# Attention scores transposed and taken by pairs of query tiles, with the low halves on GpSimd

## The reference, cut to what matters

```
x = x + tanh(((modulated x) @ weight @ aux1 @ aux2) + bias)
Q2, K2 = x @ Wq2 + bq2, x @ Wk2 + bk2
V = concat(cond, x) @ Wv + bv
A = softmax(Q2 @ K2.T / 16) - alpha * softmax(Q1 @ K1.T / 16)
x = x + quantised_ffn(A @ V)
```

## Time and profile before

| | |
|---|---|
| median of 3 runs | 240.14 us (239.92 to 242.85) |
| the profiled execution's own time | 242.43 us |
| its span | 240.5 us |
| attention stage, 57.26 to 190.33 us | 133.07 us |
| TensorE busy in the span | 230.2 us (96%) |
| VectorE, ScalarE, GpSimd busy | 149.8, 121.9, 70.9 us |

### The profile page before, as it was taken

One profiled execution on the slowest core, in us unless ns is written; L12 is line 12 of the kernel. 1 busy time (PEld: TensorE's weight loads), 2 busy tenths in 40 slices (PEclk: granted clock), 3 DMA queues, 4 the chain that ended last, 5 costly groups with the idle time before them and its releaser, 6 DMA issues.

```text
span 240.5 us, 3882 instructions
## 1 busy us (share of the span) xinstructions
PE 230.2 (96%) x1455; PEld 188.7 (78%) x1455; DVE 149.8 (62%) x325; ACT 121.9 (51%) x222; POOL 70.9 (29%) x97
## 2 busy tenths in 40 slices
PE   7987999999999999999999999999999899998994
PEld 7977899988997899989999899889999544433342
DVE  0744322887466557855886546546555597999963
ACT  2567603666324444345344434445435669944932
POOL 8340910444000000480663400000000065663850
PEclk9999968999999999999999999999999999999999
DMA  5990019000000000000000000000000000000044
GB/s 182 301 337 13 0 34 329 24 0 3 0 0 0 3 0 0 3 0 3 3 0 0 3 0 0 3 1 0 3 0 3 1 0 0 3 0 0 0 172 177
DMA packets 7105, 9.61 MB, mean 40 GB/s; under 512 B 800, under 2 KB 4912, under 8 KB 7088
## 3 DMA queue, kind: packets, MB, share of 16 engines
q1 hardware_dynamic: 6624, 9.11, 11.0%
q10 hardware_dynamic: 144, 0.26, 0.4%
q0 software_dynamic: 320, 0.01, 0.1%
HBM read 7.28 MB, written 2.10 MB: 39 GB/s over the span
## 4 chain that ended last, share of the span: by engine, by line
PE 81%; DVE 10%; issue 4%; ACT 2%; POOL 2%; POOLq 0%; DVEq 0%
PE ps L1017 54%; PE ps L1164 6%; DVE hmax L860 4%; PE ps L1347 3%; PE ps L1064 3%; PE ps L1001 2%; PE ps L1299 2%; DVE hid L855 2%; PE ps L1047 1%; PE ps L1204 1%; PE ps L1373 1%; PE ps L1009 1%; PE ps L1103 1%; POOL hid L980 1%; DVE hi L902 1%
## 5 line engine op out<-in xcount | busy, mean ns | idle before, releaser
L1017 PE MATMUL ps<-vh,pth 128*128 128x256 f32 x128 | 37.3, 292 | 0.3 <-DVE ptl L605 0.3
L1017 PE MATMUL ps<-vl,pth 128*128 128x256 f32 x128 | 36.1, 282 | 0.0
L1017 PE MATMUL ps<-vh,ptl 128*128 128x256 f32 x128 | 36.1, 282 | 0.0
L480 ACT ACTIVATE prob<-ps,small 128x1024 f32<-128x1024 f32 x16 | 17.8, 1115 | 21.7 <-DVE small L750 21.7
L495 ACT ACTIVATE outT<-ps,small 128x128 f32<-128x128 f32 x32 | 10.0, 366 | 33.7 <-PE ps L1204 33.7
L1017 PE MATMUL ps<-x1h,xh 128*128 128x512 f32 x64 | 26.2, 409 | 0.0
L748 DVE TENSOR_REDUCE small<-ps 128x1 f32<-128x1024 f32 x16 | 19.6, 1222 | 10.1 <-PE ps L1017 9.9
L1017 PE MATMUL ps<-x1h,xl 128*128 128x512 f32 x64 | 25.2, 393 | 0.0
L1017 PEld LDWEIGHTS ps<-vh,pth 128*128 128x128 f32 x128 | 24.4, 191 | 0.9 <-issue 0.9
L1017 PE MATMUL ps<-x1l,xh 128*128 128x512 f32 x64 | 25.0, 390 | 0.0
L1017 PEld LDWEIGHTS ps<-vl,pth 128*128 128x128 f32 x128 | 24.5, 191 | 0.0
(11 more groups left out here) (226 smaller groups left out, 557.2 us busy)
## 6 DMA issues: line engine op xcount, KB each, us to landing
result<-yst SPq DMA_DIRECT2D x8, 256.0 KB, 2.1
xn<-in_x SPq DMA_DIRECT2D x4, 256.0 KB, 5.9
xn<-in_x SPq DMA_DIRECT2D x2, 512.0 KB, 9.2
wdn<-in_L_ffn_w_down SPq DMA_DIRECT2D x1, 704.0 KB, 7.4
wgn<-in_L_ffn_w_gate SPq DMA_DIRECT2D x1, 640.0 KB, 4.4
wun<-in_L_ffn_w_up SPq DMA_DIRECT2D x1, 640.0 KB, 5.3
a<-in_L_ffn_aux_weight SPq DMA_DIRECT2D x2, 256.0 KB, 6.2
wvf<-in_L_cond_Wv SPq DMA_DIRECT2D x1, 512.0 KB, 10.8
```

Of the source, the lines that this page charges most:

```text
L480: act.activation(prob[:, j % 2, :], ps[:, 2 * (j % 2):2 * (j % 2) + 2, :], ACT.Exp, bias=col("nb", j % 2), scale=ATT_SCALE, accum_out=col( ...
L1017: last = pe.matmul(dst, a, b, start=(n == 0), stop=(n == len(passes) - 1))
```

## The change

Two query tiles make a pair (`QP` = 256 queries, `NP` = 8 pairs). Scores are computed transposed: keys on the partitions, queries along the columns, so that no transpose of the probabilities is needed. The softmax subtracts one maximum for each query, which now lies along the columns: DVE first takes the maximum over the eight key tiles (`key_max`), two transposes bring it to the queries (`key_max_T`), DVE finishes it (`query_max`), two transposes of a broadcast column spread it over the partitions (`spread_top`), and DVE subtracts it from the scores into SBUF (`distances`). ACT takes the exponential there in place and copies the high half; GpSimd subtracts for the low half, except for three of the four pieces of the last pair, which DVE does. The sum of the exponentials comes from a column of ones beside the values. All 16 values are made before the loop. The quantisation of the weights on GpSimd is cut in six parts, behind the low halves of pairs 2 to 6.

```diff
+            def scores(g, between={}):
+                for k in range(TPB):
+                    if g >= 1 and k % 2 == 0:
+                        pe.wait_ge(d_ready, 4 * (g - 1) + k // 2 + 1)
+                    if k in between:
+                        between[k]()
+                    t = slice(k * P, (k + 1) * P)
+                    last = three_passes(ps[:, k // 2, k % 2 * QP:(k % 2 + 1) * QP],
+                                        [(x1h[:, b, c, t], x1l[:, b, c, t], queries(xh, g, c), queries(xl, g, c))
+                                         for c in range(DC)])
+                    if k % 4 == 3:
+                        last.then_inc(s_ps, 1)
...
+            for g in range(1, NP):
+                scores(g, {4: lambda: do_extra(("out", g - 2))} if g >= 2 else {})
+                if g in after_scores:
+                    do_extra(after_scores[g])
+                attend(g - 1, {(0, 15): lambda: key_max_T(g), (1, 3): lambda: spread_top(g)})
+                if g in after_attend:
+                    do_extra(after_attend[g])
+            for item in at_end[:-2]:
+                do_extra(item)
+            attend(NP - 1, {(1, 12): lambda: do_extra(("tile", 0))})
+            do_extra(("tile", 1))
```

The work of ScalarE and VectorE:

```diff
+            def softmax(g):
+                for k in range(4):
+                    act.wait_ge(d_ready, 4 * g + k + 1)
+                    act.activation(prob[:, 2 * k:2 * k + 2, :], prob[:, 2 * k:2 * k + 2, :], ACT.Exp,
+                                   scale=ATT_SCALE).then_inc(p_ready, 1)
+                    if k == 0 and g >= 2:
+                        act.wait_ge(o_ps, 2 * (g - 1))
+                    act.wait_ge(p_ready, 4 * g + k + 1)
+                    copy(pth[g % 2][:, 2 * k:2 * k + 2, :], prob[:, 2 * k:2 * k + 2, :], pth_ready)
...
+            def key_max(g, h):
+
+                dve.wait_ge(s_ps, 2 * g + h + 1)
+                ins = dve.tensor_reduce(kmax[:, h, :], flat(ps[:, 2 * h:2 * h + 2, :]).rearrange("p (k q) -> p q k", k=4),
+                                        X_AXIS, ALU.max)
+                if h:
+                    link(ins)
+                    dve.tensor_tensor(kmax[:, 0, :], kmax[:, 0, :], kmax[:, 1, :], ALU.max).then_inc(kmax_ready, 1)
...
+                key_max(g, 1)
+                if g in after_scores:
+                    extra_lo(after_scores[g])
+                query_max(g)
+                distances(g)
+                if g >= 2:
+                    out_max(("out", g - 2))
+                attention_out(g - 1)
+                if g <= IC:
+                    ffn_weight_scales((g - 1) // 2, (g - 1) % 2)
```

After its last softmax ScalarE reads up 0, and then the items of `at_end`. GpSimd:

```diff
+            def prob_lo(g):
+                for k in range(4):
+                    if low_half_on(g, k) == "pool":
+                        pool.wait_ge(pth_ready, 4 * g + k + 1)
+                        pool.tensor_tensor(ptl[:, g % 2, 2 * k:2 * k + 2, :], prob[:, 2 * k:2 * k + 2, :],
+                                           pth[g % 2][:, 2 * k:2 * k + 2, :].bitcast(F32),
+                                           ALU.subtract).then_inc(ptl_ready["pool"], 1)
+
+            for g in range(NP):
+                prob_lo(g)
+                for m in {2: [0], 3: [1], 4: [2], 5: [3], 6: [4, 5]}.get(g, []):
+                    k, part = m // 2, m % 2
+                    n = (IC if k < 2 else DC) // 2
+                    ffn_weight(k, range(part * n, (part + 1) * n), n)
```

More of the change, by code:

```diff
@@ L116, in build_block, with low_half_on, low_halves @@
               (3, 4, "act", "act")]
+    def low_half_on(g, k):
+        return "dve" if g == NP - 1 and k > 0 else "pool"
+    def low_halves(g, k, engine):
+        return sum(low_half_on(i, j) == engine for i in range(g + 1) for j in range(4) if (i, j) <= (g, k))
     def rounded_upto(piece, engine):
@@ L484, in probT_hi @@
[L484 to L492, removed]
+                copy(vh[:, v, 0:D], ps[:, bank, 0:D], vh_ready)
+            def softmax(g):
[7 more added lines that the diff above has]
+                    copy(pth[g % 2][:, 2 * k:2 * k + 2, :], prob[:, 2 * k:2 * k + 2, :], pth_ready)
@@ L502, in extra_read @@
                     query_hi(item[1], item[2], ps[:, MISC, :])
-                elif item[0] == "value":
-                    value_hi(item[1], MISC)
+                elif item[0] in ("out", "tile"):
+                    out_hi(item)
                 else:
@@ L753, in probT_lo @@
[L753 to L766, removed]
@@ new lines, in _ @@
+            dve.wait_ge(x1T_ready, DC * NH)
+            rank_one_vectors()
+            for v in range(NT):
+                if v == 4:
+                    key_max(0, 0)
+                    rank_one_columns()
+                    key_max(0, 1)
+                value_lo(v, value_bank(v))
+                if v == 9:
+                    dve.wait_ge(vl_ready, 2)
+                    query_max(0)
+            distances(0)
+            extra_lo(after_scores[0])
+            key_max(1, 0)
+            dve.wait_ge(vl_ready, NT)
@@ L831, in _ @@
+            attention_out(NP - 1, (0,))
+            out_max(("out", NP - 2))
+            attention_out(NP - 1, (1,))
+            for t in range(2):
+                out_max(("tile", t))
+            dve.wait_ge(am_ready, NP + 1)
+            dve.tensor_reduce(col("am"), amax[:, 0:NP + 1], X_AXIS, ALU.max).then_inc(am_ready, 1)
             dve.wait_ge(amT_ps, 1)
@@ new lines, in rank_column @@
+            def rank_column(m):
+                if m == 0:
+                    pe.wait_ge(vxc_ready, 2 * B)
+                    pe.wait_ge(vl_ready, 2)
+                for k in range(DC):
+                    for n, (w, v) in enumerate(((wvf[:, DC + k, :], "vx"), (wvf[:, k, :], "vc"))):
+                        last = pe.matmul(ps[:, MISC, 2 * m:2 * m + 2], w[:, m * P:(m + 1) * P], col(v, k * B, B),
+                                         start=(k == 0 and n == 0), stop=(k == DC - 1 and n == 1))
+                return last
```

410 lines of the change are left out of this document (189 added, 221 removed).

## The result

| | before | after |
|---|---|---|
| median of 4 runs each | 240.03 us (239.06 to 242.85) | 244.69 us (242.58 to 245.89) |
| profiled execution: own time, span | 242.43, 240.5 us | 245.36, 243.6 us |
| from the first value behind layer 0 to the spread (L1308, now L1356) | 57.37 to 190.33 | 57.45 to 193.40 |
| that stage | 132.96 us | 135.95 us |
| from the spread to the end of the span | 50.17 us | 50.20 us |

The kernel became slower: 1.0181 times the time before, 95% interval 1.0128 to 1.0233. The forecast was 238.6, with a range to 242.5. What lies behind the spread didn't change, so in the two profiled executions the stage holds the difference, 2.99 of 3.1 us of span: forecast to end at 187.1, or 188.8 with the clock, it ended at 193.40. (The medians differ by 4.7 us. No trace places the other 1.7.) Now I go from the sums to the gaps, in the order in which the prediction went.

A forecast was written before the change was run, and what follows sets the result against it. TensorE's work plus few gaps bounds the kernel. The stage was to save 3.2 to 3.3 us, the clock's fall cost 1.7: -1.6, so 240.8 profiled, and 238.6 against the 240.14 median; range 235.5 to 242.5.

The forecast's parts named there:

- So in the middle TensorE has no gap: Pairs 1 to 6: the other engines feed TensorE in time, DVE summing to 8.7 to 10.7 us of 12.4 to 13.8.
- the rule that the prediction put aside: The skill's rule that DVE instructions with two SBUF inputs contend with GpSimd's SBUF reads; set aside, priced as rival 4.
- the fall: Near the last `attend`, TensorE's clock falls to half after the 3.45 us gap, costing 1.7 us, between 0 and 2.4.
- the offset: Profiled execution before lies 2.29 us above the runs' median; 240.8 profiled after therefore became a forecast of 238.6.
- Rows 8: Trace rows before: DVE's L749 starts at 118.11 inside POOL's 117.86 to 118.26, takes 0.16; cited against the skill's rule.
- rival 4: Joining maximum and two tiny DVE sums wait behind GpSimd's quantising: at most 4 us, say 2, total 240.6; chance 0.06.
- 1, the clock stays up: At the gap before out 6, TensorE's clock doesn't fall: total 236.9 us; chance 0.20.
- 2, no gap at the end: Before out 6 no gap, since ACT's pieces take 0.9 us or less: total 233.5 us; chance 0.07.
- 3, the strided maximum dear: `key_max` at 2.44 us instead of 1.22 stalls TensorE, +3.6 us, 242.2; over 250 if dearer; chance 0.14.
- 5: GpSimd's low halves come late; at 2.5 us instead of 1.28, seven pairs wait 1.5: total 249 us; chance 0.07.
- 6: Score matmuls of 256 columns cost their weight load too, 0.14 us each, +8 us: total 246.6; chance 0.03.
- TensorE's work: In the attention stage, TensorE's work falls by a net 8.5 us, to 122.3 from 130.8.

The follow-up runs named there:

- e1: Against the kernel after, ACT reads gate 0, gate 1 and up 0 between the second and third softmax piece: stage 130.31 us, 0.9946 times before.
- e10: Against the kernel after, up 0 gets bank 0 and the last tile bank 7, ACT's order kept: stage 132.67 us, own time 239.63 us.
- e2: Against the kernel after, 14 matmuls without use put into the gap ahead of out 6: stage 134.45 us, 1.0053 times before.
- e8: Against the kernel after, e1, e5's order, later rank-one sums and an earlier first query together: stage 127.04 us, 0.9769 times before.
- e5: Against the kernel after, e1 and, besides, down 0 and down 1 ahead of out 6: stage 129.16 us, 0.9847 times before.

## Why the prediction was wrong

**The step that failed** is "So in the middle TensorE has no gap." It followed each engine's load through a pair, and found margins, but it asked only at the end which bank an item waits for. Out 4 and out 5 wait for gate 0 and gate 1 just as out 6 waits for up 0: same bank, same place in ACT's program, behind the softmax of the pair. Here it costs 1.03 us each (e1 and e10 show it from two sides). At the end it was forecast, at 3.45 us, and measured, at 3.44. The second thing that failed is the rule that the prediction put aside, below.

**The account of the error.** The spread came 4.6 us later than forecast. Start: `scores(1)` ended at 85.4 for 84.0, +1.4; half of it is the wait of the rank-one columns, 0.74, and the rest are steps that the sum left out, seven of 0.08 to 0.11 us where one kind of matmul follows another. Middle: `scores(7)` ended at 170.4 for 166.2, of which 1.4 came from the start; of the other 2.8, 2.06 are out 4 and 5 and 0.31 is `key_max_T` of pair 6; the last 0.4 no run takes apart. End: 23.0 us from there to the spread, for 20.95 + 1.7, +0.35, with 0.27 for `key_max_T` of pair 7 and the fall 0.26 cheaper than forecast. The medians missed by 6.1. The other 1.5 is the offset: the profiled execution of before was 2.3 above its median and that of after only 0.7. The scatter of layer 0 can do that, but no run shows that it did.

**The rule that I put aside.** The prediction says that the trace does not agree with it. Rows 8 were no test: the DVE instruction overlapped the last 0.15 us of GpSimd's, and lasted 0.16. The rows of L718 and L722 above are one, and TensorE waited 0.74 + 0.30 us for such instructions, 1.0 of rival 4's "at most 4, say 2". The Trainium skill, SBUF — State Buffer, section Who interferes with whom, says of DVE in a mode that takes both ports: "Whoever issues first gets the shared pair for the whole instruction; the other fully blocks". It counts a DVE instruction with two SBUF inputs, as L718 is, among those that contend with GpSimd. The trace agrees, with 152 ns that became 1057. The same section counts `tensor_scalar` among the instructions that can use the shared ports when their operands meet its conditions, and L722, with one SBUF input, was held as well (1.22 us for 0.224).

**The rivals.** 1, the clock stays up: no; it fell in both profiles of the kernel after, and stayed up to the spread when the idle stretch was filled (e2). 2, no gap at the end: no. 3, the strided maximum dear: no, 1220 ns. 4: partly, as said. 5 and 6: no; the fourth low half kept its margin, and score matmuls of 256 columns go at the pace of `attend`'s, with the work at about 122 us. The rivals that made the kernel slower than before (3 to 6) had 0.30 together, and but for a part of 4 they did not come about: what made it slower was in none of them.

**What was right**: TensorE's work, the prices of all new instructions, the waits at the query, at out 6 and at the end, and the fall of the clock with its size. The forecast named the gaps' mechanism and missed two of its places. With most of its waits gone (e8) the change brings the 8.5 us of work back as 5.9 us of stage.

## What to carry to other kernels

Where items share a buffer in a fixed order, go through every item and ask what its previous tenant's reader has ahead of it in its own queue; what was true for the last was true for two more here. Tiny instructions on a path deserve a look at what the neighbour engine runs at that moment, since their own duration says nothing then. And when a big saving of work comes back as nothing, list the waiting engine's gaps by size before blaming what was moved: here the place of three reads in ACT's program was worth 5.6 us of the stage (4.2 of waits, and 1.5 of low clock that came back behind the stage), and the engine that makes the low halves, which looked like the bold part of the change, 0.2.

## What the runs showed of the hardware

I had not expected that a DVE instruction on four columns can take 1057 ns for 152. It isn't the only one: the four instructions of the weight scales on 128x3 (L804) took 0.17, 0.84, 0.84 and 0.83 us, where the kernel before has 0.17 for each. The second of them starts 0.46 us after a low half on GpSimd (two instructions of 1.26 in one row), and ends at 110.91, just where the first of the two must end (109.61 + 1.26 = 110.87):

```profile
110.07 0.84 DVE L804 TENSOR_SCALAR wsc<-wmax 128x3 f32<-128x3 f32 x1
```

```profile
109.61 2.52 POOL L1005 TENSOR_TENSOR ptl<-prob,pth 128x512 fp32r<-128x512 f32 x2
```

It goes the other way too. In e1 DVE's joining maximum starts first, takes its usual time, and GpSimd's instruction, which begins 0.03 us later, takes 0.65 us for 0.41 (0.66 at the same place in e5 and e8):

```profile
153.87 0.42 DVE L751 TENSOR_TENSOR downT<-downT 128x256 f32<-128x256 f32 x1
```

```profile
153.90 0.65 POOL L998 TENSOR_SCALAR wgn<-wun 128x256 bf16<-128x256 f32 x1
```

The second thing is how loosely the clock is tied to gaps. Two gaps of 1.03 us in the middle brought no fall. With out 6 waiting 1.50 us (e1) and 1.51 (e10), and nearly the same gaps at the very end, the clock fell behind the spread in the first and not at all in the second; with about 0.3 at out 6 it fell in e8 and not in e5. In the first stage, layer 0, the clock of one and the same kernel falls in one run and not in another. Which of the short gaps brings a fall isn't settled by these runs; the long one was followed by a fall each time it stood open, in six profiles.
